# Fused embedding, attention and expert block: three maxima pairs in each group, softmax sums inverted on a turned column, two-input products on GpSimd

## Chip, cores and metric

One Trainium2 chip, one of its cores. The metric is the device time of one execution in microseconds (us). TensorE (PE) multiplies, VectorE (DVE), ScalarE (ACT) and GpSimd (POOL) work elementwise, SyncE (SP) issues the transfers. Matmul results go to PSUM, eight banks of 512 float32 columns in each partition; GpSimd works on SBUF alone.

## The reference

For each of 16 batch elements, 1101 rows of 128 features (1024 image tokens and 77 text tokens) go through an attention layer and a feed-forward layer with experts:

```
h = concat(tok(x) + position, txt(x_txt))                  # 16 x 1101 x 128
n = layernorm(h)
for head in 8 heads of 64:
    p = softmax(q k^T / 8)                                 # 1101 x 1101
    o = p v
h = h + concat(o) @ head_kernel
f = layernorm(h) * scale + bias
shared = (silu(a) * b) @ shared_out                        # a, b = f @ shared_in
group = argmax of 2 gates; top 2 of its 4 experts, softmax weights
out = h + shared + sum_e weight_e * (h_expert @ expert_out[e]) + biases
```

## The kernel before

**Items and groups.** The program runs over items, b from -1 to 16. Item b does the attention of batch element b, the layers behind it (`post`) for element b - 1, and the embedding, norm and first projections (`prep`) for element b + 1. Attention takes 108 steps: 4 pairs of heads, 3 chunks of queries (`CHUNKS`, 368 columns), 9 tiles of 128 keys. Three steps are a group, so an item has 36 groups and a pair of heads 9. All other work is cut into units (`("max", p, j, c)`, `("qk", ...)`, `("expert", t, g)`, and so on) that `plan` puts into groups once, before the program is written; there is no dynamic order.

**A group on each engine.** PE runs the row phase (three scores, with the group's maxima pairs between them, `row_phase`), then the weighting (`weigh`) of the three steps of the group before, then the group's sum and units. A score is 8 matmuls in 2 banks: three products of high and low parts and a fourth that subtracts the row's maximum (`q_max` with `k_one`). ACT takes two exponentials of each score into `probs`, a ring of 6 steps. POOL adds the probabilities up into `sums`, so that 8 additions make the denominator of a chunk; PE's `sum` unit adds over the partitions with a matrix of ones, which leaves the same number in all 64 rows of a head. DVE reduces the maxima pairs (`part_max`), does the group's inversions and products, then its units.

**Maxima.** Ahead of each pair of heads, 27 maxima pairs (tile of queries x chunk of keys) give every row's maximum. Each pair is one matmul for each head, in 2 banks, and one DVE reduction (two where the banks don't lie side by side). Then `neg_max` is turned by PE (`maxrow`), copied by DVE (`max_rows`) and taken by four transfers of SP's queue into `q_max`; the first score of the pair waits for `max_loaded`.

**Banks.** Seven banks (`work`) rotate over all units in program order: a score or a maxima pair takes two, any other unit one. `wait_banks` lets a unit start when what held its banks has been drained.

**Sums.** `invert` takes the reciprocal of the 368 equal-by-rows columns in four parts, two in each of the two groups after the sum; `divide` multiplies `heads_t` by it on DVE.

## Time and profile before

| | |
|---|---|
| median of 3 runs | 5006.49 us (5006.3 to 5009.66) |
| the profiled execution's own time | 5007.34 us |
| its span (first to last instruction) | 5005.5 us |
| PE busy | 4551.0 us, 91% |
| DVE busy | 3373.4 us, 67% |
| ACT busy | 2186.9 us, 44% |
| POOL busy | 2771.3 us, 55% |
| DMA, mean | 10 GB/s |

Busy time is the union of an engine's instructions. Matmuls are pipelined and their ends are modelled: two matmuls on the two halves of the array are 0.33 us each in the records while a new pair starts every 0.17 us, and a PE that is called busy may be waiting for part of it. The chain of work that ended last tells who was waited for: it goes back from the last instruction, at each step to what released it.

### The profile page before, as it was taken

Reading aid. Unit: us, or ns where it says so; the run is one execution under the profiler, and the core shown is the slowest. Engines: PE = TensorE matmul, PEld = TensorE weight load, DVE = VectorE, ACT = ScalarE, POOL = GpSimd, SP = SyncE. Lnnn points to the kernel's source line nnn. Section 1 sums busy time; section 2 is a strip of 40 time slices with the busy share of each in tenths; the row PEclk is TensorE's granted clock in tenths of the full one; section 3 lists DMA queues with packets and bytes.
Section 4 is the critical chain, followed back from the end, with each engine's and each line's share of the span. In section 5 each row is a group of like instructions: output and inputs, shape, how many; then the busy total and the mean of one; then the engine's idle time right before and its main releaser. Section 6 shows DMA issues by size and latency. Waiting matters only on the chain.

```text
span 5005.5 us, 89640 instructions
## 1 busy us (share of the span) xinstructions
PE 4551.0 (91%) x32741; PEld 3138.4 (63%) x32741; DVE 3373.4 (67%) x6632; ACT 2186.9 (44%) x5256; POOL 2771.3 (55%) x1609
## 2 busy tenths in 40 slices
PE   5999999999999999999999999998999999999997
PEld 4666666666666666666666666666666666666666
DVE  5667766666666667667676666766666666666765
ACT  2554444444444444444444444444444444444442
POOL 1775555655556555565555655556555565655561
PEclk7999999999999999999999999999999999999998
DMA  1000000000000000000000000000000000000000
GB/s 40 12 6 7 6 16 6 11 7 6 16 6 11 9 13 7 6 11 11 11 7 6 16 6 11 7 6 16 6 10 7 6 16 6 11 7 14 3 1 15
DMA packets 42928, 48.85 MB, mean 10 GB/s; under 512 B 26256, under 2 KB 34311, under 8 KB 42503
## 3 DMA queue, kind: packets, MB, share of 16 engines
q1 hardware_dynamic: 42503, 43.12, 2.8%
q8 instruction: 274, 4.49, 0.4%
q14 instruction: 151, 1.24, 0.1%
HBM read 23.45 MB, written 19.09 MB: 8 GB/s over the span
## 4 chain that ended last, share of the span: by engine, by line
PE 64%; DVE 27%; issue 4%; ACT 2%; SPq 1%; DMA 1%; POOL 0%; DVEq 0%; ACTq 0%; POOLq 0%
PE o_ps L795 20%; PE work L759 16%; DVE part_max L923 10%; PE work L731 8%; DVE h_out L987 4%; PE work L778 4%; PE work L690 3%; PE work L681 2%; PE work L714 2%; PE work L661 2%; PE work L670 2%; DVE sums L1007 2%; DVE heads_t L1017 2%; PE work L720 2%; DVE hid L971 1%
## 5 line engine op out<-in xcount | busy, mean ns | idle before, releaser
L1168 POOL TENSOR_TENSOR sums<-sums,probs 128x736 f32<-128x736 f32 (+3 forms) x1344 | 2369.7, 1763 | 1370.8 <-ACT probs L879 1243.3
L879 ACT ACTIVATE probs<-work 128x368 f32<-128x368 f32 (+3 forms) x3456 | 1419.0, 478 | 1727.1 <-PE work L759 1636.2
L923 DVE TENSOR_REDUCE part_max<-work 128x2 f32<-128x736 f32 (+3 forms) x1474 | 1299.7, 917 | 173.1 <-PE work L778 164.8
L795 PE MATMUL o_ps<-probs,values 128*64 128x368 f32 (+1 forms) x6912 | 1229.2, 492 | 0.4 <-ACT probs L879 0.2
L759 PE MATMUL work<-q_hi,k_hi 64*128 64x368 f32 (+3 forms) x3456 | 683.1, 386 | 198.4 <-DVE part_max L923 98.1
L778 PE MATMUL work<-k_hi,q_hi 64*128 64x368 f32 (+3 forms) x3456 | 654.5, 375 | 149.4 <-DVE part_max L923 112.8
L795 PEld LDWEIGHTS o_ps<-probs,values 128*64 128x64 f32 (+1 forms) x6912 | 458.3, 140 | 528.5 <-issue 398.1
L987 DVE SCALAR_TENSOR_TENSOR h_out<-work,comb,h_out 128x128 f32<-128x128 f32 x1152 | 404.3, 351 | 471.9 <-PE work L731 434.8
L1164 POOL TENSOR_TENSOR sums<-probs 128x736 f32<-128x736 f32 (+1 forms) x192 | 336.4, 1752 | 623.6 <-ACT probs L879 571.1
L759 PEld LDWEIGHTS work<-q_hi,k_hi 64*128 64x128 f32 (+1 forms) x3456 | 334.6, 181 | 459.5 <-issue 199.6
L759 PE MATMUL work<-q_max,k_one 64*128 64x368 f32 (+3 forms) x3456 | 593.2, 330 | 0.0
L759 PE MATMUL work<-q_hi,k_lo 64*128 64x368 f32 (+3 forms) x3456 | 593.0, 330 | 0.0
L759 PE MATMUL work<-q_lo,k_hi 64*128 64x368 f32 (+3 forms) x3456 | 592.6, 330 | 0.0
L778 PEld LDWEIGHTS work<-k_hi,q_hi 64*128 64x128 f32 (+1 forms) x3456 | 352.1, 184 | 319.0 <-issue 135.3
L1007 DVE RECIPROCAL sums<-sums 128x92 f32<-128x92 f32 (+1 forms) x768 | 499.1, 691 | 8.8 <-ACT sums L838 8.8
L759 PEld LDWEIGHTS work<-q_lo,k_hi 64*128 64x128 f32 (+1 forms) x3456 | 338.3, 184 | 1.4
L759 PEld LDWEIGHTS work<-q_max,k_one 64*128 64x128 f32 (+1 forms) x3456 | 338.0, 183 | 1.5
L759 PEld LDWEIGHTS work<-q_hi,k_lo 64*128 64x128 f32 (+1 forms) x3456 | 337.1, 183 | 1.4
L945 DVE TENSOR_TENSOR k_lo<-work,k_hi 128x368 fp32r<-128x368 f32 (+1 forms) x192 | 102.7, 535 | 221.6 <-ACT k_hi L834 221.6
L731 PE MATMUL work<-down_hi,hid_hi 128*128 128x512 f32 x576 | 245.5, 426 | 0.0
L829 ACT COPY values<-work 128x256 f32<-128x256 f32 x288 | 105.3, 373 | 290.7 <-PE work L661 290.7
L731 PE MATMUL work<-down_lo,hid_hi 128*128 128x512 f32 x576 | 229.5, 398 | 0.0
(191 smaller groups left out, 5276.1 us busy)
## 6 DMA issues: line engine op xcount, KB each, us to landing
resid_rows<-h_in SPq DMA_DIRECT2D x16, 576.0 KB, 2.8
h_out<-resid_rows SPq DMA_DIRECT2D x16, 576.0 KB, 3.7
h_in<-in_pe_table_dram SPq DMA_DIRECT2D x16, 512.0 KB
out_dram<-h_out SPq DMA_DIRECT2D x16, 512.0 KB
q_max<-max_rows SPq DMA_DIRECT2D x128, 4.0 KB
q_max<-max_rows SPq DMA_DIRECT2D x128, 0.3 KB
counts<-in_x_dram SPq DMA_DIRECT2D x16, 116.0 KB, 2.8
out_raw<-n_expert_out_weight_dram SPq DMA_DIRECT2D x1, 1024.0 KB
```

The lines of the kernel that those rows point to most:

```text
L690: mm = nc.tensor.matmul(w[:, 0:D], heads_t[:, p, j * P:(j + 1) * P], wo[:, p, :], start=(p == 0), stop=(p == PAIRS - 1))
L731: mm = nc.tensor.matmul(w, h[:, k2, cols], wt[:, k2, g * EG * D:(g + 1) * EG * D], start=(n == 0), stop=(n == len(ops) - 1))
L759: mm = nc.tensor.matmul(work[0:n, banks.of[b, ("score", s)][i], 0:cw], k, asks[r][half, c0:c0 + cw], start=(m == 0), stop=(m == 3))
L778: mm = nc.tensor.matmul(work[0:n, banks.of[b, u][i], 0:cw], q_hi[r][half, j * P:j * P + n], k_hi[r][half, c0:c0 + cw], start=True, stop=True)
L795: mm = nc.tensor.matmul(o_ps[64 * i:64 * i + 64, 0:cw], values[0:n, t, h * DH:(h + 1) * DH], probs[0:n, s % NP, i, 0:cw], start=(t == 0), ...
L829: nc.scalar.copy(values[:, j, half * HALF:(half + 1) * HALF], w[:, 0:HALF]).then_inc(drained[k], 1)
L879: nc.scalar.activation(probs[0:n, s % NP, i, 0:cw], work[0:n, banks.of[b, ("score", s)][i], 0:cw], ACT.Exp, scale=DH ** -0.5).then_inc(pro ...
L923: nc.vector.tensor_reduce(part_max[0:n, :, j, c:c + 1], work[0:n, ka:ka + 2, 0:keys], AX.X, ALU.max).then_inc(max_taken, 1)
L987: ins = nc.vector.scalar_tensor_tensor(out=o, in0=w[:, e * D:(e + 1) * D], scalar=comb[:, t, g * EG + e:g * EG + e + 1], in1=o, op0=ALU.mu ...
L1007: nc.vector.reciprocal(inverse[:, cols], inverse[:, cols]).then_inc(s_chain, 1)
L1164: nc.gpsimd.tensor_tensor(acc, probs[:, (s - 1) % NP, :, 0:cw], probs[:, s % NP, :, 0:cw], ALU.add).then_inc(sums_done, 1)
L1168: nc.gpsimd.tensor_tensor(acc, acc, probs[0:n, s % NP, :, 0:cw], ALU.add).then_inc(sums_done, 1)
```

## The change

`plan` puts three maxima pairs into each of the nine groups of the pair of heads before, in the order score, score, maxima, score, maxima, maxima. The six projections of a pair of heads are made at the end of the pair before the last (`projected`), and `maxrow` moves from the eighth to the last group of a pair, ahead of these projections; the wait for `max_loaded` stands ahead of the fourth matmul pair of the first score, no longer ahead of its first. A sum is filled for 384 columns; DVE turns it in blocks of 32 x 32 (`turned`), inverts the 12 columns that hold each block's first row, and turns them back, each spread over 32 columns, into `spread`. The product with `heads_t` (`scale`), the low part of the normalised rows (`split_flat`) and that of the hidden rows (`split_hid`) are made on POOL; the high parts on ACT, for the normalised rows all at once in group 7. ACT's copy of the sum is gone. The output projections, the statistics, the gate, the ranking and the weights of the experts have other groups. The experts' additions, which were chained four by four, alternate between two units.

```diff
-PROJ = [1, 1, 2, 2, 2, 3, 3, 3, 4]
-STATS, NORMAL, TURN, GATE, WEIGHTS, COUNT = 4, 5, 6, 8, 9, 10
+PROJ = [0, 1, 1, 2, 2, 2, 3, 3, 3]
+STATS, NORMAL, TURN, GATE, COUNT = 4, 5, 6, 7, 10
+CHOOSE, RANK, WEIGHTS = (7, 1), (8, 0), (9, 0)
...
+        mine, g = p >= 1, PAIR * ((p - 1) % PAIRS)
+        if (attn and mine) or (prep and not mine):
+            for n, u in enumerate(maxima(p)):
+                put(g + n // GROUP, u)
+            put(g + PAIR - 1, ("maxrow", p))
+        mine, g = p >= 2, PAIR * ((p - 2) % PAIRS) + PAIR - 1
+        if (attn and mine) or (prep and not mine):
+            for u in projections(p):
+                put(g, u)
...
+            units += [("shared", t) for t in range(3 * c, 3 * c + 3)]
+            units += [("expert", t, g) for g in range(2) for t in range(3 * c, 3 * c + 3)]
...
+    return [u for kind in "SSMSMM" for u in [next(of[kind], None)] if u]
...
+                if m == 3 and s % STEPS == 0:
+                    pe.wait_ge(max_loaded, 64 * (PAIRS * b + p + 1))
...
+        def add_expert(b, u, e):
+            if e == 0:
+                wait_drained(dve, b, ("expert", t, 0) if g else ("shared", t))
+                wait_filled(dve, b, u)
+            else:
+                dve.wait_ge(s_chain, added[b, u, e - 1])
...
+        def invert(b, q):
+            wait_filled(dve, b, ("sum", q))
+            nc.vector.transpose(turned[:], work[:, k, 0:PADDED]).then_inc(drained[k], 1)
+            wait_drained(dve, b, ("sum", q))
+            then(nc.vector.reciprocal(inverse[:], turned[:].rearrange("p (a n) -> p a n", n=32)[:, :, 0]))
+            wait(dve, heads_scaled, n - 1)
+            nc.vector.transpose(spread[:, q % 2, :].rearrange("p (a n) -> p a n", n=32),
+                                inverse[:].unsqueeze(2).broadcast_to((P, PADDED // 32, 32))).then_inc(spread_ready, 1)
...
+        def scale(b, q):
+            pool.wait_ge(heads_out, n + 1)
+            pool.wait_ge(spread_ready, n + 1)
+            nc.gpsimd.tensor_tensor(o, spread[:, q % 2, 0:cw], o, ALU.mult).then_inc(heads_scaled, 1)
```

**On PE, a row phase.** Before, in the second group of an item: a score is the four rows with `q_hi`, `q_lo`, `k_lo` and `k_one` (x2 for the two heads), a maxima pair one row with `k_hi,q_hi`.

```order
L759 MATMUL work<-q_hi,k_hi 128x368 x2
L759 MATMUL work<-q_lo,k_hi 128x368 x2
L759 MATMUL work<-q_hi,k_lo 128x368 x2
L759 MATMUL work<-q_max,k_one 128x368 x2
L778 MATMUL work<-k_hi,q_hi 128x368 x2
L759 MATMUL work<-q_hi,k_hi 128x368 x2
L759 MATMUL work<-q_lo,k_hi 128x368 x2
L759 MATMUL work<-q_hi,k_lo 128x368 x2
L759 MATMUL work<-q_max,k_one 128x368 x2
L778 MATMUL work<-k_hi,q_hi 128x368 x2
L778 MATMUL work<-k_hi,q_hi 128x366 x2
L759 MATMUL work<-q_hi,k_hi 128x368 x2
```

After, in the first group of an item, from its second score on:

```order
L772 MATMUL work<-q_hi,k_hi 128x368 x2
L772 MATMUL work<-q_lo,k_hi 128x368 x2
L772 MATMUL work<-q_hi,k_lo 128x368 x2
L772 MATMUL work<-q_max,k_one 128x368 x2
L791 MATMUL work<-k_hi,q_hi 128x368 x2
L772 MATMUL work<-q_hi,k_hi 128x368 x2
L772 MATMUL work<-q_lo,k_hi 128x368 x2
L772 MATMUL work<-q_hi,k_lo 128x368 x2
L772 MATMUL work<-q_max,k_one 128x368 x2
L791 MATMUL work<-k_hi,q_hi 128x368 x2
L791 MATMUL work<-k_hi,q_hi 128x366 x2
L808 MATMUL o_ps<-probs,values 64x366 x6
```

A maxima pair stood behind each score, with four or five pairs in such a group; now the first stands behind the second score and there are three.

**On PE, the hand-off of the maxima row.** Before: the turned maxima, and the first rows of the whole group of scores that follows it.

```order
L795 MATMUL o_ps<-probs,values 64x366 x6
L674 MATMUL work<-ident,neg_max 18x128
L759 MATMUL work<-q_hi,k_hi 128x366 x2
L759 MATMUL work<-q_lo,k_hi 128x366 x2
L759 MATMUL work<-q_hi,k_lo 128x366 x2
L759 MATMUL work<-q_max,k_one 128x366 x2
L759 MATMUL work<-q_hi,k_hi 128x366 x2
```

After: the turned maxima, then the projections (the first 8 of their 18 rows)

```order
L808 MATMUL o_ps<-probs,values 64x366 x6
L686 MATMUL work<-ident,neg_max 18x128
L682 MATMUL work<-yt_hi,wqk_hi 128x368
L682 MATMUL work<-yt_lo,wqk_hi 128x368
L682 MATMUL work<-yt_hi,wqk_lo 128x368
L682 MATMUL work<-yt_hi,wqk_hi 128x368
L682 MATMUL work<-yt_lo,wqk_hi 128x368
L682 MATMUL work<-yt_hi,wqk_lo 128x368
L682 MATMUL work<-yt_hi,wqk_hi 128x368
L682 MATMUL work<-yt_lo,wqk_hi 128x368
```

and their last rows, with the first score that needs the row's transfer, in its fourth matmul pair:

```order
L682 MATMUL work<-yt_hi,wqk_hi 128x366
L682 MATMUL work<-yt_lo,wqk_hi 128x366
L682 MATMUL work<-yt_hi,wqk_lo 128x366
L772 MATMUL work<-q_hi,k_hi 128x368 x2
L772 MATMUL work<-q_lo,k_hi 128x368 x2
L772 MATMUL work<-q_hi,k_lo 128x368 x2
L772 MATMUL work<-q_max,k_one 128x368 x2
```

Between the turned row and its first use there were three scores, a weighting and the units of a group; now there are the projections and three rows of a score.

**On DVE, a sum.** Before, the reciprocals and the product, between maxima of three groups:

```order
L923 TENSOR_REDUCE part_max<-work 128x2 x4
L1007 RECIPROCAL sums<-sums 128x92 x2
L923 TENSOR_REDUCE part_max<-work 128x2 x3
L1007 RECIPROCAL sums<-sums 128x92
L1007 RECIPROCAL sums<-sums 128x90
L1017 TENSOR_TENSOR heads_t<-sums,heads_t 128x366
```

After, with the maxima ahead of the sum and the maxima row's copy behind the next group's:

```order
L1042 STREAM_TRANSPOSE turned<-work 128x384
L1044 RECIPROCAL inverse<-turned 128x12
L1046 STREAM_TRANSPOSE spread<-inverse 128x384
L936 TENSOR_REDUCE part_max<-work 128x2 x3
L936 TENSOR_REDUCE part_max<-work 78x2 x3
L944 TENSOR_REDUCE neg_max<-part_max 128x18
L962 CAST max_rows<-work 18x128
```

Four reciprocals and a product became two transposes and a short reciprocal, all in the group of the sum; the product stands on POOL.

## Rows read from the trace of the kernel before

**Rows 1.** The page, part 4: chain that ended last, by engine, shares of the span.
```profile
PE 64%; DVE 27%; issue 4%; ACT 2%; SPq 1%; DMA 1%; POOL 0%; DVEq 0%; ACTq 0%; POOLq 0%
```

**Rows 2.** Windows: full item, clean group, heavy group, groups 5 and 6; length, then busy times.
```profile
947.63:1252.55 304.92, 280.10 (x2045) 193.01 (x2043) 209.40 (x407) 136.14 (x327) 173.27 (x101) 0.99 0.03 9
1091.13:1099.04 7.91, 7.91 (x58) 5.84 (x57) 4.51 (x12) 3.27 (x8) 5.27 (x3) 1.00 0.01 2
1044.74:1056.73 11.99, 9.02 (x66) 5.66 (x66) 8.28 (x16) 3.47 (x8) 3.50 (x2) 1.00 0.01 1
981.27:993.69 12.42, 10.99 (x94) 7.36 (x93) 9.91 (x26) 6.44 (x17) 9.25 (x7) 1.00 0.01 1
```

**Rows 3.** Chain in the clean group: start us, length us, piece.
```profile
1090.91 2.21 PE work L759 x24
1093.12 2.00 PE o_ps L795 x12
1095.12 1.59 PE work L731 x6
1096.71 2.11 PE work L714 x12
```

**Rows 4.** Chain in the heavy group, as above.
```profile
1048.58 1.66 DVE part_max L923 x2
...
1053.63 0.62 PE work L681 x4
1054.25 0.64 PE work L720 x4
1054.89 0.22 PE work L722 x2
1055.12 1.41 PE work L731 x6
```

**Rows 5.** Timeline of the heavy group: start, length, instruction, idle time before and releaser.
```profile
1049.56 0.44 PE L778 MATMUL work<-k_hi,q_hi 64*128 64x368 f32 x2 [1.69 <-DVE part_max L923]
...
1050.75 0.85 ACT L879 ACTIVATE probs<-work 128x368 f32<-128x368 f32 x2 [2.12 <-PE work L759]
```

**Rows 6.** Chain of the whole run: one set of six projections.
```profile
3165.42 3.23 PE work L670 x18
```

**Rows 7.** Chain around 1014 us: nine gate products, two records each.
```profile
1014.07 2.11 PE work L702 x18
```

**Rows 8.** Groups of instructions by line: busy us, mean ns, idle before.
```profile
L1168 POOL TENSOR_TENSOR sums<-sums,probs 128x736 f32<-128x736 f32 (+3 forms) x1344 | 2369.7, 1763 | 1370.8 <-ACT probs L879 1243.3
...
L923 DVE TENSOR_REDUCE part_max<-work 128x2 f32<-128x736 f32 (+3 forms) x1474 | 1299.7, 917 | 173.1 <-PE work L778 164.8
...
L1007 DVE RECIPROCAL sums<-sums 128x92 f32<-128x92 f32 (+1 forms) x768 | 499.1, 691 | 8.8 <-ACT sums L838 8.8
...
L1107 DVE TENSOR_TENSOR hid_lo<-hid,hid_hi 128x384 fp32r<-128x384 f32 x96 | 98.5, 1050 | 114.1 <-ACT hid_hi L898 113.8
...
L1017 DVE TENSOR_TENSOR heads_t<-sums,heads_t 128x368 f32<-128x368 f32 (+1 forms) x192 | 128.0, 667 | 2.0
...
L1066 DVE TENSOR_TENSOR rank<-rank,beats 128x27 f32<-128x27 f32 (+2 forms) x48 | 8.6, 179 | 1.1
```

**Rows 9.** Tile hid_lo, its writer: least, median, longest ns.
```profile
L1107 DVE TENSOR_TENSOR hid_lo<-hid,hid_hi x96: 494/940/2129, 427.4 to 4985.2; 128x384 fp32r<-128x384 f32 x96
```

**Rows 10.** Timeline around one hand-off of the maxima row.
```profile
941.93 0.27 PE L674 MATMUL work<-ident,neg_max 128*18 128x128 f32 x1
...
942.92 0.21 DVE L949 CAST max_rows<-work 18x128 fp32r<-18x128 f32 x1
...
945.43 0.76 SPq L1223 DMA_DIRECT2D q_max<-max_rows  x1
...
947.33 0.44 PE L759 MATMUL work<-q_hi,k_hi 64*128 64x368 f32 x2 [0.58 <-DMA q_max<-max_rows]
```

**Rows 11.** Tile q_max: its matmuls, first and last start.
```profile
L759 PE MATMUL work<-q_max,k_one x3456: 320/327/508, 104.1 to 4902.3; 64*128 64x368 f32 x128, 64*128 64x366 f32 x64
```

237 lines of the change are left out of this document (123 added, 114 removed).

## Prediction

> **What bounds the kernel now.** I read the chain of work that ended last first [rows 1]: 64% of the span is matmuls and 27% is VectorE (DVE). POOL (GpSimd) and ACT (ScalarE) hardly appear. So TensorE (PE) is the engine that should set the pace, and for a quarter of the time it waits, directly or not, for DVE. The windows come next [rows 2]: one full item (a batch element) takes 304.92 us; PE is called busy for 280.10 of them, but overlapping matmul records hide lost time, so I worked out PE's pace from the chain instead.
>
> In an undisturbed group of three steps the chain is nothing but PE [rows 3]: 24 score matmuls 2.21 us, 12 weighting records 2.00, one expert unit 1.59, an "up" set of four units 2.11; the group takes 7.91. A group that has a softmax sum, four or five maxima pairs and leftovers of the feed-forward part takes 11.99 [rows 2], and its chain shows DVE: maxima in a row before PE may go on [rows 4]. In the same group PE stood idle 1.69 us for a reduction of the maxima [rows 5]: seven PSUM banks rotate, and a score or maxima pair cannot start until DVE has emptied the banks that it gets.
>
> PE's pace per full item, from the chain's pieces: scores 36 x 2.21 = 79.6; weighting 36 x 2.00 = 72.0; 108 maxima pairs at a score pair's 2.21/12 = 0.18, 19.9; sums 12 x 0.62 = 7.4, shared 9 x (0.64 + 0.22) = 7.7, experts 18 x 1.41 = 25.4 [rows 4]; up 6 x 2.11 = 12.7 [rows 3]; query and key projections 4 x 3.23 = 12.9 [rows 6]. The small ones (values, output projection, gate, turns, embedding) are some 200 records; at 2.11/18 = 0.117 us [rows 7], a little more for the wide ones, I take 25, an estimate. Sum 263 us. The item takes 305: about 42 us of each item is waiting, and that is what this change can win.
>
> **The change part by part.** *Sums inverted on a turned column.* Removed per sum: four reciprocals of 0.691 us and a product of 0.667 on DVE [rows 8], 3.4 us, 12 times an item: 41 us of DVE. Added: two transposes of 384 columns and a reciprocal of 12. The trace has no DVE transpose. From below it is nearest to a one-source pass from PSUM: 736 columns take 0.917, so 384 take 0.48. From above, by the slowest DVE row, the reciprocal's 0.691 for 92 columns, it would be 2.9. I take 0.5, since a transpose computes nothing, and 1.3 per sum with the short reciprocal and its two waits: 16 us an item. At the upper end the three would cost 6 us, more than what they replace, 31 us of DVE an item added; that end is kept for the range. A scale to that: the Trainium skill, Vector Engine (DVE) Microarchitecture Reference, "The reshape front-end and per-opcode configuration", says that a transpose keeps up one element per cycle per lane, and by it the price would stay by the lower end; no row here shows it. ACT loses its copy of the sum.
>
> *Products moved to GpSimd.* The split of the hidden rows costs DVE 1.050 us each, 6 an item [rows 8], though its fastest instance is 0.494 and its slowest 2.129 [rows 9]: some 0.5 us each is waiting. With the split of the normalised rows DVE is rid of about 9 us an item. GpSimd gets 21 products an item. Its additions take 1.763 for 736 columns, so 384 take 0.92: 19 us more on top of 173.27 [rows 2, 8]. 192 of 280 us is 69% busy, and the ring of six probability buffers lets it lag by two groups. I cost it at nothing outside groups 5 to 8, where the additions meet the norm's root and three splits; the cover gone, it would be its whole 19 us. Groups 5 and 6 take 12.42 us now [rows 2] for matmuls that need under 11; I leave 4 us an item for groups 5 to 8. The Trainium skill, SBUF — State Buffer, "Who interferes with whom", has the rule behind the spread: a DVE instruction with two SBUF inputs and a GpSimd instruction that reads SBUF exclude each other for a whole instruction. By it DVE sheds the waits as well as the work, and GpSimd's products are never blocked; if instead the spread were only chance, DVE would save 3 us less an item, which is off the path. Rows 9 agree with the rule.
>
> *Three maxima pairs in each group.* Before, some groups held five or six pairs and others none. Now DVE has 3 x 0.917 = 2.8 us in each, and with the above its total falls from 209.40 to about 209 - 41 + 16 - 9 = 175 of 280 us, and only one group stays above its PE time: maxima, rank, maxima row and six low halves are some 9 us of DVE, an estimate, in a group of 8.3. The 42 us of waiting should mostly go. The order score, score, maxima, score, maxima, maxima costs a little: scores end at 0.74 and 1.47 us, their exponentials (0.85 a pair, [rows 5]) at 1.6 and 2.45, the first maxima pair is filled at 1.65 and reduced at 2.6, and the last maxima pair needs one bank of each. PE would be there at 2.57. With semaphores that is 0.15 us, 36 times: 5 us an item.
>
> *The maxima row is turned later.* It was in group 7 of a pair, with a whole group of scores before its use; now it is in group 8, with six projections after it. From the transpose on PE (941.93) to the first score that may use the loaded row (947.33) the trace shows 5.4 us, of which DVE's copy was 0.5 late behind reciprocals [rows 10]; so 4.9 to 5.4. PE covers 0.2 for the transpose, 3.23 of projections [rows 6] and three of four score passes, 0.55, since the wait now stands ahead of the fourth: 4.0. A wait of 0.9 to 1.4 us is new, say 1.15, four times an item, 4.6. Behind it are queued all further scores, and ACT and GpSimd starve. In the first pair of an item the rank chain (12 small instructions, 0.179 each and a wait behind most, [rows 8]) stands on DVE between the maxima and the copy: 2 us more. A clock dip after the longest of these waits: 1. Together 8 us an item. The SyncE queue issues the same four transfers and waits for nothing new ahead of them.
>
> *Gate chain earlier, expert additions interleaved.* The counts come a group earlier, so PE no longer waits for them at group 10; interleaving takes the semaphore time out of the additions. Both only let DVE finish sooner and are inside the 42 us.
>
> Sum for a full item: 263 + 5 + 8 + 4 = 280, instead of 305, 25 less. There are 14 such items, 350 us. Scores run from 104.1 to 4902.3 [rows 11]; the other two items, which lack the feed-forward part or the preparation, take the remaining 530 us and save the same 8%, 43. They get 10 more if the average full item is, like most windows beside this one, a little over 305. The lead-in gets one more projection (+3), the tail's additions save some 5. 400 + 5 = 405. The profiled execution took 5007.34 us (span 5005.5), 0.85 above the median of 5006.49: 5007 - 405 = **4600 us**.
>
> **The rivals.** (a) *All waiting goes, the hand-off is hidden.* For it: clean groups run at PE's pace today [rows 3]. Against it: the 4.0 us of cover against 4.9. Items of 263 to 270: 4330 to 4470. (b) *DVE's lost work is all that comes back.* If the waits by banks stay, whatever the number of maxima, only what leaves the path by name is won: reciprocals, product and half of the additions, some 5% of the chain by their busy time, 250 us, less 130 of new hand-off waits: 4870; with half of the bank waits gone, 4700 to 4870. The slow transpose falls here too: at 2.9 us it puts 31 us of DVE back, a third of it on the path, 4760. For it: eleven units still share seven banks. (c) *The hand-off decides, slower than before.* If SyncE's queue holds the four transfers back behind a store or a load, PE stands still in every pair. The rest saves 33 us an item; four hand-offs have to cost over 8 us each, against 1.15 by [rows 10], so their landing would have to be at 12 us instead of 5. (d) *No change*: what is taken from DVE was slack, PE waits for something else. Against it: 27% of the chain.
>
> **How the numbers follow.** The forecast, full items of 276 to 286 and so 4530 to 4690, gets 0.52; (a) 0.20; (b) 0.20; (c) 0.04; (d) 0.04. The range takes half of (a) and the nearer half of (b): 4440 to 4790. Within 0.2% is what a measurement of this kernel cannot tell from no change; faster 0.93, same 0.03, slower 0.04.
>
> **What would show it.** In the profile after: reciprocals and products gone from DVE, two transposes near 0.5 us (over 1 speaks for b); DVE near 175 us an item; PE's waits for the maxima's reductions down from hundreds to tens; a wait of about 1 us for the maxima row's transfer some 64 times, longer each fourth time; DVE's share of the chain under 15%. The forecast is wrong if the small units' 25 us is far off, if ACT, now asked for exponentials every 7 us with casts between, holds the banks instead of DVE, or if GpSimd's lag stops the exponentials.

## The result, and the profile after

The changed kernel took 4797.31 us (median of 4, 4795.19 to 4797.62) against 5008.07 for the kernel before on the same chip (5006.3 to 5010.81): ratio 0.9578, 95% interval 0.9561 to 0.9594. That is 211 us faster; 405 were forecast, and 4797 lies above the range of 4440 to 4790.

| | before | after |
|---|---|---|
| span of the profiled execution | 5005.5 us | 4795.7 us |
| PE busy | 4551.0, 91% | 4533.5, 95% |
| DVE busy | 3373.4, 67% | 3053.8, 64% |
| ACT busy | 2186.9, 44% | 2103.8, 44% |
| POOL busy | 2771.3, 55% | 3087.1, 64% |

The chain that ended last, by engine, answers to [rows 1]:

```profile
PE 78%; DVE 11%; SPq 3%; DMA 3%; ACT 2%; issue 2%; POOL 0%; DVEq 0%; ACTq 0%; POOLq 0%
```

DVE fell from 27% to 11%, SP's queue and its transfers came up from 2% to 6%. The windows answer to [rows 2]: a full item, then its group 8, which ends in the first hand-off of the maxima row. Columns: start:end, length, then busy time of PE, PE's loads, DVE, ACT, POOL, granted clock, DMA share, GB/s.

```profile
911.84:1204.43 292.59, 279.56 (x2043) 192.15 (x2043) 189.52 (x376) 131.05 (x318) 192.86 (x121) 0.99 0.03 10
970.27:984.59 14.32, 8.74 (x63) 6.25 (x63) 11.74 (x28) 5.40 (x13) 6.94 (x5) 0.98 0.01 2
```

The items lie at 291.8 to 295.9 us where 280 were forecast. POOL has the 192 us that the prediction gave it; DVE has 189.5, not 175. The groups by line answer to [rows 8]; the last number is the engine's idle time just before, and what ended it.

```profile
L936 DVE TENSOR_REDUCE part_max<-work 128x2 f32<-128x736 f32 (+3 forms) x1484 | 1326.4, 919 | 489.7 <-PE work L791 453.1
...
L791 PE MATMUL work<-k_hi,q_hi 64*128 64x368 f32 (+3 forms) x3456 | 653.1, 369 | 94.1 <-DVE part_max L936 54.8
...
L772 PE MATMUL work<-q_max,k_one 64*128 64x368 f32 (+3 forms) x3456 | 594.5, 333 | 63.5 <-DMA q_max<-max_rows 63.5
...
L1201 POOL TENSOR_TENSOR heads_t<-spread,heads_t 128x368 f32<-128x368 f32 (+1 forms) x192 | 188.1, 980 | 262.2 <-DVE spread L1046 262.0
```

DVE now stands idle 489.7 us ahead of reductions of the maxima, where it was 173.1 before. PE's idle time ahead of the maxima pairs was 149.4 us before and is 94.1 now, and 63.5 are new at the wait for the maxima row. Taking all of PE's idle time that a reduction ended, it fell from 251 to 66 us in the whole run. That is only the idle time that the records show: since a matmul pair is 0.33 to 0.44 us long in them and the next starts 0.17 after it in an even flow, a wait of 0.1 to 0.3 us leaves no idle time, only a wider spacing of starts. Two places in the trace are worth reading. First a group with nothing but scores, maxima and weighting (group 5 of the item), PE's timeline, and DVE's first reduction in it:

```profile
948.92 0.44 PE L772 MATMUL work<-q_hi,k_hi 64*128 64x368 f32 x2
949.19 0.34 PE L772 MATMUL work<-q_lo,k_hi 64*128 64x368 f32 x2
...
950.20 0.34 PE L772 MATMUL work<-q_max,k_one 64*128 64x368 f32 x2
950.37 0.34 PE L791 MATMUL work<-k_hi,q_hi 64*128 64x368 f32 x2
950.60 0.39 PE L772 MATMUL work<-q_hi,k_hi 64*77 64x368 f32 x2
...
950.74 0.93 DVE L936 TENSOR_REDUCE part_max<-work 128x2 f32<-128x736 f32 x1 [0.66 <-PE work L791]
...
951.33 0.91 PE L791 MATMUL work<-k_hi,q_hi 64*128 64x368 f32 x4
...
951.82 0.43 PE L791 MATMUL work<-k_hi,q_hi 64*128 64x366 f32 x2
952.18 2.08 PE L808 MATMUL o_ps<-probs,values 128*64 128x368 f32 x12
954.18 0.44 PE L772 MATMUL work<-q_hi,k_hi 64*128 64x366 f32 x2
```

From the first score to the weighting it takes 952.18 - 948.92 = 3.26 us, then 2.00 for the weighting. The prediction had 2.21 + 3 x 0.18 + 0.15 = 2.90 and 2.00. None of PE's records here has an idle time before it; the 0.36 are in the spacing. The first maxima pair follows its score after 0.17, as in an even flow. The third score starts 0.23 behind that pair, and the third maxima pair (951.82, the second half of the `x4` row) 0.48 behind the second (951.33): it shares a bank with the first, whose reduction ends at 950.74 + 0.93 = 951.67.

Second, group 8, all engines:

```profile
969.07 3.00 POOL L1206 TENSOR_TENSOR flat_lo<-normed,flat_hi 128x384 fp32r<-128x384 f32 x3
972.02 5.48 POOL L1192 TENSOR_TENSOR sums<-sums,probs 128x732 f32<-128x732 f32 x3
972.15 1.65 DVE L1078 TENSOR_TENSOR e_sel<-e_sel,e_tmp 128x36 f32<-128x36 f32 x1
...
975.13 0.39 PE L791 MATMUL work<-k_hi,q_hi 64*78 64x366 f32 x2 [3.08 <-DVE part_max L936]
...
979.46 0.28 DVE L962 CAST max_rows<-work 18x128 fp32r<-18x128 f32 x1
...
982.10 0.76 SPq L1275 DMA_DIRECT2D q_max<-max_rows  x1
983.97 0.61 PE L772 MATMUL work<-q_max,k_one 64*128 64x368 f32 x2 [2.50 <-DMA q_max<-max_rows]
```

DVE works on the choice of the experts from 969.27 to 974.04, in six instructions. Before, the first of them took 0.82 us too and the others 0.16 to 0.20 each; now the fourth and fifth take 1.05 and 1.65, and the third 0.91. Behind them stand the maxima's reductions, so PE is idle for 3.08; behind those the ranking, then the copy of the maxima row, so PE is idle for another 2.50. The tile `e_sel` over the whole run (least/median/longest ns):

```profile
L1075 DVE TENSOR_TENSOR e_sel<-logits,g_on x16: 186/1045/1779, 386.6 to 4725.3; 128x36 f32<-128x36 f32 x16
L1078 DVE TENSOR_TENSOR e_sel<-e_sel,e_tmp x16: 195/1652/1676, 387.7 to 4725.5; 128x36 f32<-128x36 f32 x16
```

and the wait for the maxima row in the item above, on PE:

```profile
L772 PE MATMUL work<-q_max,k_one 64*128 64x368 f32 x128 | 22.5, 342 | 5.1 <-DMA q_max<-max_rows 5.1
```

### The profile page after: what moved, and what is told of

The parts are those of the page before. It is cut to its first block, busy times and chain, and to the rows that moved or that the text cites. A ratio compares the mean times of both kernels' runs of the same rounds, so it can differ in the third digit from the quotient of the medians.

```text
span 4795.7 us, 88965 instructions
## 1 busy us (share of the span) xinstructions
PE 4533.5 (95%) x32741; PEld 3105.8 (65%) x32741; DVE 3053.8 (64%) x6047; ACT 2103.8 (44%) x5112; POOL 3087.1 (64%) x1945
## 4 chain that ended last, share of the span: by engine, by line
PE 78%; DVE 11%; SPq 3%; DMA 3%; ACT 2%; issue 2%; POOL 0%; DVEq 0%; ACTq 0%; POOLq 0%
PE work L772 22%; PE o_ps L808 22%; PE work L742 8%; PE work L791 8%; PE work L725 4%; PE work L701 3%; DVE part_max L936 3%; DMA q_max<-max_rows 2%; PE work L692 2%; DVE h_out L1006 2%; PE work L673 2%; SPq L1273 2%; PE work L731 2%; ACT normed L868 1%; SPq L1275 1%
## 5 line engine op out<-in xcount | busy, mean ns | idle before, releaser
L889 ACT ACTIVATE probs<-work 128x368 f32<-128x368 f32 (+3 forms) x3456 | 1398.7, 479 | 1394.6 <-PE work L772 1362.5
L936 DVE TENSOR_REDUCE part_max<-work 128x2 f32<-128x736 f32 (+3 forms) x1484 | 1326.4, 919 | 489.7 <-PE work L791 453.1
L808 PE MATMUL o_ps<-probs,values 128*64 128x368 f32 (+1 forms) x6912 | 1213.0, 486 | 0.0
L791 PE MATMUL work<-k_hi,q_hi 64*128 64x368 f32 (+3 forms) x3456 | 653.1, 369 | 94.1 <-DVE part_max L936 54.8
L772 PE MATMUL work<-q_max,k_one 64*128 64x368 f32 (+3 forms) x3456 | 594.5, 333 | 63.5 <-DMA q_max<-max_rows 63.5
L1006 DVE SCALAR_TENSOR_TENSOR h_out<-work,comb,h_out 128x128 f32<-128x128 f32 x1152 | 388.3, 349 | 338.4 <-PE work L742 313.7
L791 PEld LDWEIGHTS work<-k_hi,q_hi 64*128 64x128 f32 (+1 forms) x3456 | 342.0, 181 | 269.1 <-ACT probs L889 141.9
L772 PEld LDWEIGHTS work<-q_max,k_one 64*128 64x128 f32 (+1 forms) x3456 | 331.8, 181 | 84.1 <-DMA q_max<-max_rows 82.9
L1201 POOL TENSOR_TENSOR heads_t<-spread,heads_t 128x368 f32<-128x368 f32 (+1 forms) x192 | 188.1, 980 | 262.2 <-DVE spread L1046 262.0
L1042 DVE STREAM_TRANSPOSE turned<-work 128x384 f32<-128x384 f32 x192 | 111.9, 583 | 254.1 <-PE work L692 253.6
L877 ACT COPY heads_t<-o_ps 128x368 f32<-128x368 f32 (+1 forms) x192 | 89.3, 465 | 339.5 <-PE o_ps L808 339.5
```

Of the source, the lines that this page charges most:

```text
L772: mm = nc.tensor.matmul(work[0:n, banks.of[b, ("score", s)][i], 0:cw], k, asks[r][half, c0:c0 + cw], start=(m == 0), stop=(m == 3))
L791: mm = nc.tensor.matmul(work[0:n, banks.of[b, u][i], 0:cw], q_hi[r][half, j * P:j * P + n], k_hi[r][half, c0:c0 + cw], start=True, stop=True)
L808: mm = nc.tensor.matmul(o_ps[64 * i:64 * i + 64, 0:cw], values[0:n, t, h * DH:(h + 1) * DH], probs[0:n, s % NP, i, 0:cw], start=(t == 0), ...
L889: nc.scalar.activation(probs[0:n, s % NP, i, 0:cw], work[0:n, banks.of[b, ("score", s)][i], 0:cw], ACT.Exp, scale=DH ** -0.5).then_inc(pro ...
L936: nc.vector.tensor_reduce(part_max[0:n, :, j, c:c + 1], work[0:n, ka:ka + 2, 0:keys], AX.X, ALU.max).then_inc(max_taken, 1)
L1006: ins = nc.vector.scalar_tensor_tensor(out=o, in0=work[:, k, e * D:(e + 1) * D], scalar=comb[:, t, g * EG + e:g * EG + e + 1], in1=o, op0= ...
```

## The experiments

Fifteen kernels ran beside the kernel before. "After" is the changed kernel. Below, the length of a group is the time from its first ready score to that of the next group, mean of nine items; its first part ends with the last weighting matmul and is 4.42 us in an undisturbed group of after. Times stand as measured; each ratio is to the kernel before on the same chip, known to about 0.15%, so two of these kernels that differ by less than some 10 us can't be told apart.

**e1: the gate's chain half a group to a group later.**

```diff
-CHOOSE, RANK, WEIGHTS = (7, 1), (8, 0), (9, 0)
+CHOOSE, RANK, WEIGHTS = (8, 1), (9, 0), (9, 1)
```

> The changed kernel with the expert chain moved off the maxima row's path: the choice of the group behind the units of group 8, the ranking in group 9, the weights behind group 9's units. Theory A (the chain, stretched and standing ahead of the maxima and of the row's copy, is what makes group 8 take 14.3 us): group 8 falls to about 9.6 us like the other hand-off groups, group 9 grows by under 1; 15 items x 4 us = 60 us less, about 4735. Theory B (the chain only shifts, DVE is full in group 9 too): group 9 takes what group 8 gives, within 15 us of 4797.

4823.59 us, ratio 0.9637 (0.9622 to 0.9651), 26 us slower than after and slower than either theory allowed. Group 8 did fall from 14.3 to 9.9, but group 10 rose from 8.1 to 14.6: the chain of weights met GpSimd's additions there (three in a row from 994.18, 5.48 us). The chain that ended last in group 10:

```profile
994.53 1.45 DVE e_tmp L1107
...
996.11 1.74 DVE comb L1110
...
998.94 0.47 PE work L791 x2
```

So the jam belongs to the small DVE chain beside GpSimd; this move only carried it to another group with maxima.

**e2 and e3: reductions over half the columns**, in after and in before. The maxima are taken over half of each chunk; everything else is unchanged.

```diff
-            keys = min(CHUNKS[c][1], T - CHUNKS[c][0])
+            keys = min(CHUNKS[c][1], T - CHUNKS[c][0]) // 2
```

> The changed kernel with each maxima reduction reading half of its columns (this leaves half of the keys out of the row maximum). It takes about 0.4 us off each of 1728 reductions, some 45 us of DVE an item. Theory A (outside the hand-offs PE's own pace now sets the time, and my sum for that pace was too small): 1 to 2 us an item in group 8, so 4765 to 4790. Theory B (small waits for banks that DVE has not emptied are still what an item loses): 8 us an item or more, under 4675.

> The kernel before with the same halved reductions (half of the keys left out of the row maximum). Both theories: DVE's reductions were waited for, so far more than in the changed kernel: about 4850 to 4900. If it is within 40 us of 5007, the reductions were not what PE waited for, and the gain of the change came from elsewhere.

After fell to 4691.89 (0.9371, 0.9356 to 0.9387), before to 4700.57 (0.9388, 0.9374 to 0.9402). Both expectations were off: after lies between its two theories, and before gained two to three times what was expected. Halved reductions are worth 306 us to before and 105 to after. In after the gain is 0.2 us in every group (first part 4.42 to 4.21), and none in group 8 (14.3). With cheap maxima the two kernels are within 9 us of each other: nearly all of what the change gains are waits for DVE's reductions. What stays (286 and 287 us an item) is something else; e14 goes on from here.

**e4: GpSimd's three low parts of the normalised rows in three groups** (9, 10, 11) instead of all in group 7.

```diff
-            if item.post and g == TURN + 1:
-                for c in range(3):
-                    split_flat(b, c)
+            if item.post and TURN + 3 <= g <= TURN + 5:
+                split_flat(b, g - TURN - 3)
```

> The changed kernel with GpSimd's three products for the normalised rows, which now run back to back in group 7 just as DVE chooses the expert group, put one each behind the additions of groups 9, 10 and 11. Theory A (those products shut out DVE's small two-input instructions, 1.65 us instead of 0.20 for one): the choice takes 1.7 us instead of 4.8, the maxima of group 8 are no longer late, 3 us an item, about 4752. Theory B (GpSimd's additions would shut them out just as well): within 12 us of 4797.

4799.73 us, 0.9586 (0.9572 to 0.9601), no difference to after. Theory A was right on the choice of the experts and wrong on the time. The tile `e_sel` in e4:

```profile
L1078 DVE TENSOR_TENSOR e_sel<-e_sel,e_tmp x16: 195/197/198, 384.9 to 4728.1; 128x36 f32<-128x36 f32 x16
...
L1086 DVE TENSOR_TENSOR e_sel<-e_sel,e_max x16: 195/1550/1621, 390.3 to 4729.0; 128x36 f32<-128x36 f32 x16
```

L1078, unchanged in itself, falls from 1652 to 197 ns once GpSimd's products are gone from group 7 and its additions no longer queue behind them (in after an addition starts at 972.02, beside L1078's 972.15): that settles that GpSimd's work stretched it. But now L1086 of the ranking, which ran in 0.20 in after, takes 1.55. Group 8 is 13.4, and groups 9 and 10 take 0.6 and 0.5 more.

**e5: ranking behind the copy of the maxima row.**

```diff
-CHOOSE, RANK, WEIGHTS = (7, 1), (8, 0), (9, 0)
+CHOOSE, RANK, WEIGHTS = (7, 1), (8, 1), (9, 0)
```

> The changed kernel with the ranking of the experts behind group 8's units on DVE, so behind the maxima row's copy, and its exponential on ACT in group 9; nothing else moves. Theory A (the ranking ahead of the copy is 2.5 us of the hand-off): group 8 takes 11 to 12 us instead of 14.3, 15 items: 4750 to 4765. Theory B (the ranking then holds up the maxima of group 9 and the weights those of group 10, as the late chain did): within 12 us of 4797, or slower.

4780.46 us, 0.9547 (0.9532 to 0.9562): some 16 us, less than theory A's 32 to 47. Group 8 falls to 13.1. The place of the ranking costs 1.2 us an item, a little less than the 2 that were forecast for it.

**e6: score and maxima pair in turn.**

```diff
-    return [u for kind in "SSMSMM" for u in [next(of[kind], None)] if u]
+    return [u for kind in "SMSMSM" for u in [next(of[kind], None)] if u]
```

> The changed kernel with the row phase in the order score, maxima, score, maxima, score, maxima. Theory A (behind two scores the last maxima pair waits 0.2 us for the first one's reduction, in every group, since row phase and weighting end at 4.42 us and at 4.21 with halved reductions): 36 x 0.2 us x 15 items less, about 4690. Theory B (DVE is still at the units of the group before when the first maxima pair is filled, which is what the later place covers): the wait moves to the second score, 4797 or above.

4914.81 us, 0.9818 (0.9803 to 0.9833), 117 us slower than after, as theory B had it. DVE has 17% of the chain, where it has 11% in after. Quiet groups are as fast as in after (4.41). The difference comes where DVE is still at the units of the group before when the maxima arrive: the first part is 4.87 in group 13, 5.01 in group 15, 5.00 in group 31, and group 8 takes 15.8. With the order of after the first maxima pair, and so the first reduction that later units wait for, comes a score later than here.

This order also shows what a change between scores and maxima costs PE by itself, since the second score's banks have long been free here. The last matmul pair of a score, a maxima pair and a score again, in group 2 of the item:

```profile
948.28 0.33 PE L772 MATMUL work<-q_max,k_one 64*128 64x368 f32 x1
948.44 0.34 PE L791 MATMUL work<-k_hi,q_hi 64*128 64x368 f32 x2
948.61 0.34 PE L772 MATMUL work<-q_hi,k_hi 64*128 64x368 f32 x2
948.78 0.34 PE L772 MATMUL work<-q_lo,k_hi 64*128 64x368 f32 x2
```

Each starts 0.17 behind the one before it; the score behind the first maxima pair starts 0.168 us after it in the median of 324 groups. The change costs nothing.

**e7: more of the scores ahead of the wait for the maxima row.** The first three matmul pairs of the second score too stand before the first `q_max` row.

```diff
-                    score(b, u[1])
+                    score(b, u[1], (0, 1, 2))
+                    score(b, u[1] + 1, (0, 1, 2))
+                    score(b, u[1], (3,))
+                    score(b, u[1] + 1, (3,))
```

> The changed kernel with the first three matmul pairs of the second score of a pair of heads ahead of the fourth pair of the first score, where PE waits for the maxima row. Theory A (PE waits there about 1.3 us for the transfer, nothing else): 0.5 us less at each of 64 hand-offs, 30 us less, about 4767. Theory B (the wait is for something behind, ACT's or DVE's state after the projections): no change.

4784.36 us, 0.9556 (0.9541 to 0.9572), between the theories; 11 to 13 us are at the edge of what can be told. The groups behind a hand-off fall by only 0.16 (7.67 to 7.51): what PE does earlier it later waits for. On PE and ACT behind the wait of group 18:

```profile
1056.41 0.61 PE L775 MATMUL work<-q_max,k_one 64*128 64x368 f32 x4 [0.38 <-DMA q_max<-max_rows]
1056.86 0.33 PE L794 MATMUL work<-k_hi,q_hi 64*128 64x368 f32 x2
...
1056.97 0.48 ACT L899 ACTIVATE probs<-work 128x368 f32<-128x368 f32 x1 [1.63 <-PE work L775]
...
1057.59 0.44 PE L775 MATMUL work<-q_hi,k_hi 64*128 64x368 f32 x2 [0.40 <-ACT probs L899]
```

The third score takes a bank of the first, and starts 0.14 us behind the end of the exponential that empties it (1056.97 + 0.48 = 1057.45).

**e8: expert additions chained again.**

```diff
-                if left and left[0][0][1] == u[1]:
+                for e in range(EG):
+                    add_expert(b, u, e)
+                continue
```

> The changed kernel with the four additions of an expert unit chained again, not alternating with those of the next unit. Theory A (PE's pace sets the expert groups, DVE has room): within 10 us of 4797. Theory B (DVE's additions bind there): 18 units x 4 x 0.035 us x 15 items, 38 us slower, about 4835.

4789.06 us, 0.9567 (0.9549 to 0.9585), theory A. The interleaving brings nothing that can be measured.

**e9: the last maxima pair behind the first step of the weighting.**

```diff
+            late = phase.pop() if weighs and phase and phase[-1][0] == "max" else None
...
+                if n == 0 and late:
+                    maximum(b, late)
```

> The changed kernel with the last of the three maxima pairs issued behind the first of the three weighting steps. Theory A (in every group this pair waits some 0.25 us for the bank of the first maxima pair, and PE's weighting can run meanwhile): row phase and weighting end at 4.2 us instead of 4.42, 36 x 0.22 x 15 = 120 us less, about 4680. Theory B (the 4.42 us is PE's own pace, the stall is only drawn so): no change, 4790 to 4800.

4810.22 us, 0.9606 (0.9591 to 0.962), some 13 us slower than after. PE in e9:

```profile
1005.49 0.44 PE L791 MATMUL work<-k_hi,q_hi 64*128 64x368 f32 x2
1005.86 0.84 PE L808 MATMUL o_ps<-probs,values 128*64 128x368 f32 x4
1006.63 0.43 PE L791 MATMUL work<-k_hi,q_hi 64*128 64x366 f32 x2
1006.99 1.46 PE L808 MATMUL o_ps<-probs,values 128*64 128x368 f32 x8
```

A pair costs 0.17 among its own kind, four weighting matmuls 0.67. Here the pair takes 0.37 and 0.36 until the weighting starts, the four take 0.77. The wait for the bank is gone, since the pair comes some 0.8 us behind the first one's reduction, and one more change into the weighting and one out of it cost about as much: the first part stays at 4.38 to 4.45. These are changes between matmuls on halves of the rows (64*128) and on halves of the columns (128*64). In the groups of before that have no maxima the weighting starts 0.26 us behind the last score instead of 0.17, so such a change has a price; a score and a maxima pair have the same shape.

**e10: the kernel before with the new inversion alone**, the product on GpSimd.

```diff
-                for u in item.sums[g - back] if g >= back else []:
-                    for part in range(DIV):
-                        if part // 2 == back - 1:
-                            invert(b, u[1], part)
...
+            for u in item.sums[g]:
+                invert(b, u[1])
```

> The kernel before with the turned inversion and GpSimd's product alone; the plan, the row order, the maxima and the splits stay. DVE loses 3.4 - 1.6 = 1.8 us a sum, 22 us an item. Theory A (what DVE does in its crowded groups is what PE waits for, 20 us won for 41 us of DVE with halved reductions): 10 to 14 us an item, 4810 to 4860. Theory B (the spread of the maxima is the larger part of the gain): 5 us an item or less, over 4930.

4933.92 us, 0.9848 (0.9834 to 0.9863), 73 us faster than before, theory B by a hair. DVE's share of the chain, 26%, is hardly less than before (27%).

DVE's busy time fell by 285 us, some 18 an item, and an item by about 5 us (301 instead of 306): with up to five or six pairs in a group the maxima still hold PE.

**e11: after with the low parts (`split_flat`, `split_hid`) on DVE.** On DVE the low part of the hidden rows stands behind the group's sum and ahead of its units; the three of the normalised rows stand at the end of groups 9, 10 and 11, not in group 7.

```diff
-                    split_hid(b, u[1], u[3])
...
+                    dve.wait_ge(hid_hi_ready, 3 * KC * (b - 1) + KC * u[1] + u[3] + 1)
+                    nc.vector.tensor_tensor(hid_lo[:, u[3], :], hid[:, 1, u[3], :], hid_hi[:, u[3], :],
+                                            ALU.subtract).then_inc(hid_split, 1)
```

> The changed kernel with the low parts of the normalised and the hidden rows made on DVE again. Theory A (DVE now has room outside group 8, GpSimd was not the bound either): within 15 us of 4797. Theory B (the two exclude each other at SBUF, so products on GpSimd stretch DVE's small ones and the move costs as much as it brings): 20 us or more faster.

4881.57 us, 0.975 (0.9734 to 0.9766), 84 us slower than after; neither theory had it slower. The tile `hid_lo` in e11 (least/median/longest ns):

```profile
L1148 DVE TENSOR_TENSOR hid_lo<-hid,hid_hi x96: 517/1561/2146, 419.5 to 4859.1; 128x384 fp32r<-128x384 f32 x96
```

and in after:

```profile
L1211 POOL TENSOR_TENSOR hid_lo<-hid,hid_hi x96: 993/1017/1029, 423.3 to 4775.4; 128x384 fp32r<-128x384 f32 x96
```

On DVE the product swings between 0.52 and 2.15 us, on GpSimd it takes 0.99 to 1.03. Its median on DVE, 1.56, is above that of before [rows 9], 0.94. But the place matters more than the length: two of these products (1.38 and 2.13 us, from 1064.75) stand ahead of the copy of the maxima row at the end of group 17, which takes 12.2 us instead of 9.6. In the whole run PE's weight loads wait 134.8 us for the row's transfer, where it was 82.9:

```profile
PEld work L772 <- DMA q_max<-max_rows: 134.8, 63, 4.0
```

These 52 us are most of the 84, and they would not be there with the products behind the copy, which no run has.

**e12: after with the old inversion and product on DVE**, in the group behind the sum.

```diff
-            nc.vector.transpose(turned[:], work[:, k, 0:PADDED]).then_inc(drained[k], 1)
...
+            for part in range(4):
+                cols = slice(part * CHUNK // 4, min((part + 1) * CHUNK // 4, cw))
+                ins = nc.vector.reciprocal(old[:, cols], old[:, cols])
```

> The changed kernel with the inversion as it was (ACT copy, four reciprocals, product on DVE), all in the group after the sum: 22 us more DVE an item, 3.4 us in one group of three. Theory A (with three maxima pairs in each group DVE has room for it): 2 to 4 us an item, 4830 to 4860. Theory B (the cheap inversion is the gain, whatever the spread): 10 us an item or more, 4950 and above.

5020.47 us, 1.0026 (1.0016 to 1.0037), 223 us slower than after and 0.3% slower than before, so theory B. The chain by engine:

```profile
PE 62%; DVE 25%; issue 5%; SPq 3%; DMA 2%; ACT 1%; POOL 0%; DVEq 0%; ACTq 0%; POOLq 0%
```

Group 23, 9.33 us in after, takes 15.81 (window, and PE's rows in it):

```profile
1148.30:1164.11 15.81, 10.31 (x58) 6.35 (x57) 10.55 (x23) 5.90 (x15) 7.29 (x5) 0.78 0.00 0
```

```profile
1154.63 0.59 PE L772 MATMUL work<-q_hi,k_hi 64*77 64x368 f32 x2 [5.50 <-DVE h_out L1012]
...
1156.68 3.54 PE L808 MATMUL o_ps<-probs,values 128*64 128x368 f32 x12
```

DVE has four reciprocals and the product there (1148.81 to 1153.16) ahead of four expert additions; PE is idle for 5.50 us until these have emptied a bank, and then does its weighting in 3.54 us instead of 2.0. Without the cheap inversion all other parts of the change together bring nothing in this layout: every group has maxima, so whatever makes DVE late always makes some of them late. Two things are in the 223 us that are not the inversion's own length: all four reciprocals stand in one group, where before had two in each of two, and the product, here beside a busy GpSimd, takes 1.83 us in this group.

**e13: e5, e7 and e8 in one kernel.**

> The changed kernel with the three single edits that came out a little faster: ranking behind the maxima row's copy (17 us), the second score's first passes as cover (13 us), additions chained (8 us). Theory A (they work at different places and add): about 4760. Theory B (they shorten the same wait at group 8, or are chance): 4775 to 4790.

4778.7 us, 0.9553 (0.9534 to 0.9573), theory B. By the ratios they had 16, 11 and 6 us alone and have 13 together. They do not add: group 8 is 14.0 here, where e5 alone had 13.1. Why is not shown.

**e14: reductions over an eighth of the columns** (in after; the maxima are those of the first eighth of each chunk).

```diff
-            keys = min(CHUNKS[c][1], T - CHUNKS[c][0])
+            keys = min(CHUNKS[c][1], T - CHUNKS[c][0]) // 8
```

> The changed kernel with each maxima reduction reading an eighth of its columns (seven eighths of the keys are left out of the row maximum). Theory A (with halved reductions, 4692, PE already runs at its own pace outside the hand-offs; row phase and weighting 4.21 us a group): 4660 to 4690, a group not under 4.15. Theory B (banks are still waited for): another 0.2 us a group, 4580.

4669.75 us, 0.9328 (0.9313 to 0.9344), inside theory A's range. After an eighth as after a half, the first part of a group is 4.20 to 4.25. That does not make it PE's own pace. A group of e14:

```profile
978.93 0.33 PE L791 MATMUL work<-k_hi,q_hi 64*128 64x368 f32 x2
979.22 0.19 PEld L772 LDWEIGHTS work<-q_hi,k_hi 64*128 64x128 f32 x2 [0.28 <-DVE h_out L1006]
979.23 0.43 PE L772 MATMUL work<-q_hi,k_hi 64*128 64x368 f32 x2
...
979.26 0.86 ACT L889 ACTIVATE probs<-work 128x368 f32<-128x368 f32 x2
...
980.17 0.43 PE L791 MATMUL work<-k_hi,q_hi 64*128 64x366 f32 x2
...
980.54 2.08 PE L808 MATMUL o_ps<-probs,values 128*64 128x368 f32 x12
```

The third score starts 0.30 behind the maxima pair, because its weights wait for an expert addition of DVE to empty a bank. The third maxima pair (980.17) starts 0.05 us behind the end of the second score's exponentials (979.26 + 0.86 = 980.12). So it is in 271 of the 324 groups of nine items; in after the same pair starts 0.15 us behind the first pair's reduction, in 299 of 324. Where the exponential had long ended, in 28 groups of e14, the pair follows after 0.17. From first score to weighting an undisturbed group takes 3.07 us, for fifteen matmul pairs that would be 2.51 at 0.17 each. When the reductions are short, PE waits for ACT instead.

**e15: the maxima row a group earlier.** The 27 maxima pairs go into eight groups (4, 3, 4, 3, 3, 4, 3, 3), the maxima row into the eighth, and the ninth group, with its six projections, is left as cover.

```diff
-                put(g + n // GROUP, u)
-            put(g + PAIR - 1, ("maxrow", p))
+                put(g + n * (PAIR - 1) // (NT * NC), u)
+            put(g + PAIR - 2, ("maxrow", p))
...
-    return [u for kind in "SSMSMM" for u in [next(of[kind], None)] if u]
+    return [u for kind in "SSMSMMM" for u in [next(of[kind], None)] if u]
```

> The changed kernel with its 27 maxima pairs in the first eight groups of a pair of heads (three or four in each) and the maxima row turned in the eighth, so that a whole group of scores stands between it and its use, as before. Theory A (the late hand-off costs 1.2 us four times an item, and in group 8 the ranking 2 us more): group 9, 18 and so on lose their wait, 6 us an item less, and the groups with four pairs pay 0.3 each, 4 us an item: about 4765. Theory B (four pairs in a group bring the bank waits back): 4797 or more.

4700.75 us, 0.9394 (0.9377 to 0.9411): faster than both kernels, 97 us below after, and more than was expected. Its chain, and its group 8 and the group that ends in the next hand-off (group 17, 9.6 us in after):

```profile
PE 86%; DVE 10%; issue 2%; ACT 1%; POOL 0%; DMA 0%; DVEq 0%; ACTq 0%; POOLq 0%; SPq 0%
```

```profile
956.30:966.76 10.46, 7.45 (x56) 5.52 (x56) 10.08 (x20) 4.71 (x13) 6.98 (x5) 1.00 0.01 3
...
1034.57:1042.52 7.95, 7.95 (x59) 6.14 (x59) 3.73 (x8) 5.50 (x13) 6.26 (x4) 1.00 0.01 1
```

Transfers and SP are gone from the chain. Groups 17, 26 and 35 fall from 9.6, 9.8 and 9.6 to 8.0, 7.9 and 7.4. About 1.0 us of each only moved with the maxima out of these groups (first part 4.34 to 3.32), which the groups with four pairs pay with 0.3 each (4.70 to 4.75). Group 8 falls from 14.3 to 10.3: no maxima stand behind the stretched chain any more, and PE waits once, 3.01 us for the low parts of the projections behind the ranking.

## Why the prediction was right in direction and wrong in size

**Right: what bounded before, and the prices of the parts.** Halved reductions bring the kernel before down by 306 us (e3), and DVE's share of the chain fell from 27% to 11% (under 15% was forecast). The transposes are 0.583 and 0.578 us (0.5 was taken), the short reciprocal 0.228: 1.4 us a sum where I had 1.3. The Trainium skill, Vector Engine (DVE) Microarchitecture Reference, "The reshape front-end and per-opcode configuration", has a transpose keep up one element per cycle per lane; 0.583 us for 384 columns agrees with the lower end that I took by it. GpSimd's products cost 0.98 us against 0.92 forecast, and GpSimd held up no exponential that the chain shows (POOL 0%).

**Right in total: the hand-offs and jams.** The row of maxima is waited for 63 times (some 64 were forecast), 5.1 us in the item read above, 2.50 of it in group 8; the forecast was 4.6, 2 for the ranking and 1 for the clock. For jams I had put 4 us an item into groups 5 to 8; the first parts exceed 4.42 by 6.6 us an item, 3.9 of it in group 8. Together 11.7 against 12. That the total agrees is partly luck: each of the two terms is off by over 2 us.

**Wrong, the step that failed: the waits inside the row phase.** The forecast let "the 42 us of waiting" "mostly go" and put what the new order costs at "0.15 us, 36 times: 5 us an item". PE's prices next to it hold: a maxima pair is 0.17 us (0.18 taken), three scores 2.21, the weighting 2.00. But the row phase takes 3.26 us, so 3.26 - 2.21 - 3 x 0.17 = 0.54 us of every group is waiting, 19.4 us an item and not 5. In the undisturbed groups of after it has three parts:

- 0.26: the third maxima pair waits for the first one's reduction. The prediction's sketch of the row phase had the first pair filled at 1.65 us and reduced at 2.6, with PE there for the third at 2.57. In the group read above it is filled at 1.78 and reduced at 2.75, and the third pair starts 0.15 behind that, at 2.90.
- 0.18: the third score waits for the exponential of the first one's bank, and its first matmul pairs are spaced wider behind the wait (e7 shows the wait by itself). The sketch has the exponential, ending at 1.6, but no price for it.
- 0.10: behind such a wait the last pair is 0.43 long instead of 0.33, and the weighting starts 0.36 after it instead of 0.26.

With halved reductions 0.33 of the 0.54 are left, and with an eighth no less (e2, e14): the exponentials then end last. The prediction named ACT holding the banks among its signs of being wrong, for another reason. With this the sum closes. 36 x (3.26 + 2.00) = 189.4 for scores, maxima and weighting (forecast 79.6 + 72.0 + 19.9 + 5 = 176.5), and 11.7 of hand-offs and jams; the item takes 292.6, so 91.5 remain for all other units, which the forecast had at 263 - 171.5 = 91.5 too. The item is 12.5 longer than the 280 forecast. Fourteen times 12.5 is 175 of the missing 195 us; the two shorter items and the ends were not taken apart.

**The reading of before stands, but not what was made of it.** "305 - 263" was called waiting, 42 us an item, and the pace of 263 holds by the parts above. What was wrong is that spreading the maxima and relieving DVE would take most of it. Halved reductions take only 19 us of it away (e3), and an item of after still has 19.4 + 11.7 = 31 us of waiting. The clean group of [rows 3] has no maxima and so no such wait. The quietest groups of before with three maxima pairs (first part 4.36 to 4.48 against 3.33 without any) could have shown it: more than 1 us for what I had priced at 0.70.

**Priced against the wrong thing: the row order.** Against a row phase without waits it costs; against the order in turn it gains 117 us (e6). It moves the first maxima pair away from the start of the group, where DVE is still busy with the units of the group before. The prediction compared it with no wait at all instead of with the order that it replaces.

**Wrong: DVE's total.** 189.5 us instead of 175. Some 5 us are in my pricing: neighbouring instructions overlap in the records, so the reciprocals and products filled 36 us of DVE's time in an item and not 41. Some 3 are reductions of the maxima, since 19 pairs of an item instead of 14 have banks that don't lie side by side. The rest, some 6.5, are small instructions that got longer. The change puts GpSimd's split products and additions back to back in groups 7 and 8, and there a 36-column DVE instruction of 0.20 us takes 1.65. The prediction read [rows 9] as a cost that leaves DVE together with the products. It also comes back: what stays on DVE with two SBUF inputs can now wait for a busier GpSimd. The Trainium skill, SBUF — State Buffer, "Who interferes with whom", says so too for a DVE instruction with two SBUF inputs against a GpSimd instruction that reads SBUF; I used the rule in one direction alone. e4 agrees with it: with these products out of group 7 the same instruction takes 0.197. The other half of what I took from it, that GpSimd's products are never blocked, does not follow from the rule, by which either engine can be the one that waits; the hidden rows' product took 0.99 to 1.03 us on GpSimd in after all the same. What the move to GpSimd brings is not measured cleanly: e11 loses 84 us, most of it by where its products stand.

**Rivals.** (b) gave 4700 to 4870 for the case that half of the bank waits stay, and comes nearest in the number and in the mechanism: waits for banks are 0.54 us of every group. What it had wrong is that they would be DVE's alone. (a) needed items of 263 to 270; e14, with nearly free reductions, is at 285, of which some 12 are waits at hand-offs and jams and another 12 (36 x 0.33) waits in the row phase, most of them for exponentials. (c) was off: the transfers land 4.5 us behind the copy (979.46 to 983.97), not 12.

**Left open.** How the gain divides over the parts can't be summed: undoing the inversion, the order or the splits costs 223, 117 and 84 us, twice the whole gain, because each of them decides whether the maxima arrive at an idle DVE, and the first and the last undo more than one thing; against them stands the late maxima row, which e15 puts at up to 97 us. How much of these 97 is the hand-off and how much group 8's jam was not separated further. That ACT sets the remaining 0.33 us is read from the traces; no kernel with shorter exponentials or more banks was run.

## What to carry to other kernels

When a wait for buffers is to be removed, list for each unit every engine that empties the buffers it takes, with the time at which each is done: the second to last takes over when the last is made faster, and a wait below the length of one record shows only as a wider spacing of starts. Compare with a stretch that holds the same mixture of work, since a "clean" one has none of these waits. When elementwise work moves from DVE to GpSimd, list the short two-input instructions that stay on DVE beside it, and what is queued behind them; their price is set by GpSimd's instruction, not by their own size. A value that travels PE, DVE, SP's queue, PE should be started a whole stage ahead, with the last stage kept free of work for the engine in the middle, and nothing that can be late standing ahead of its part.

## What the runs showed of the hardware

- A DVE instruction of 36 columns with two SBUF inputs takes 0.20 us alone and up to 1.65 beside back-to-back GpSimd instructions (after, e4); a 384-column one 0.52 to 2.15 (e11).
- PE goes from a score to a maxima pair and back at its even pace, 0.17 us from start to start (e6). Into the weighting it takes 0.26 (the groups of before without maxima).
- PE starts a unit 0.05 us (e14) to 0.15 us (after) behind the end of the instruction that empties its bank. The first matmul pair behind such a wait is 0.43 to 0.44 us long in the records instead of 0.33 and is followed by the next after 0.24 to 0.27 instead of 0.17 (e7, e14).
- DVE's transpose of 128 x 384 float32 takes 583 ns from PSUM and 578 ns spread from 12 columns in SBUF; a reciprocal takes 691 ns for 92 columns and 228 for 12, so inverting 12 columns between two transposes is 1.4 us against 2.8 for 368 columns.
- In group 23 of e12 the granted clock falls towards the end of PE's 5.50 us of idle time (0.67 from 1152.0 to 1154.5), is 0.53 from 1154.5 to 1160.0, about its lower level of 1.2 GHz, and is 1.00 again after that: the wait costs another 1.5 us in the weighting alone. In the same group of after it is 1.00 throughout.
